# Attention and a routed expert network on one core: expert tiles fetch their own weights, second product two tiles late, segments of 10 and 6 blocks

## The chip, the cores and the metric

The kernel runs on one core of a Trainium2 chip. A core has five engines with a queue each: PE (TensorE, matrix products), DVE (VectorE), ACT (ScalarE), POOL (GpSimd) and SP (SyncE, which here only issues transfers). Transfers issued by SP, ACT and POOL are carried out by 16 DMA engines. The metric is the device time of one execution in microseconds; lower is better.

## The reference, cut to what matters

The input x has 16 sequences ("blocks") of 512 rows of 128 numbers, 8192 rows ("tokens") in all.

```python
# 1. causal attention, 16 heads of 8
Q, K, V = x@Wq, x@Wk, x@Wv
x1 = layernorm(x + softmax(mask(Q K^T / sqrt(8))) V @ Wo + bo)
# 2. two of eight experts for each token
xn = layernorm(x1) * gamma + beta
top1, top2, their probabilities -> weights g1, g2 (g1 + g2 = 1)
y_e = gelu(xn @ W1[e] + b1[e]) @ W2[e] + b2[e]      # 128 -> 512 -> 128
# 3.
out = layernorm(x1 + x1 + g1*y_top1 + g2*y_top2)
```

Each token needs only the two experts that it is routed to, so 16384 (token, expert) rows go through the expert network.

## The kernel before, in words

**Attention.** For each of the 16 blocks one iteration of some 44 us computes scores, exponentials and values, and two to three iterations later the block's rows are normalized, routed and written. POOL writes each normalized row twice by an indirect transfer into `rows_d` in DRAM, at the place that its expert's list has reached. Each row has 128 numbers and, as number 129, where its result belongs.

**Segments.** The lists are kept for two groups of blocks ("segments"), 0 to 11 and 12 to 15. When a segment's blocks are routed, DVE works out a plan (`plan_part`): which 128 rows of `rows_d` each tile reads and which expert it belongs to. Segment 0 has 104 tiles of 128 rows, segment 1 has 40, together 144 (`NT`). Lists that don't end at 128 are filled by `pad_ends`, eight transfers of SP for each segment.

**Expert tiles.** Tile n passes the engines so. SP (`load_tile`, L461 to L473) reads the tile's row number from `plan_i` into a register (L472) and starts the transfer of 128 rows to `xs`, eight tiles ahead, into one of twelve slots; before that it waits until the slot's former tile has been sent (L471). PE transposes the tile (`turn_tile`, L1122). DVE copies the transposed tile (`turned`, L1488), and copies the expert's first weights (128 x 512) from `w1_s`, which holds those of all experts, to one of two slots `w1_t` (`weights`, L1480). PE multiplies (`first_product`, L1132, four products of 128 x 128 x 128), ACT adds the bias b1 and applies gelu (L840), PE multiplies with W2 from `w2_s` one tile later (`second_product`, L1148), DVE adds the bias b2 (`result`, L1496), and POOL sends the 128 result rows to `y_d` by an indirect transfer (`send`, L640). DVE reads the expert's number into a register twice for each tile (`expert_of`, L1473), ACT once (L834), PE once (L1140).

`w1_s` lies in the memory of the attention's keys (`kside`), `w2_s` in that of its queries (`qarea`); both are filled in block 15's iteration (`load_experts`).

**Order.** Each engine's program is one list. Tiles 0 to 85 are written between the instructions of the attention's last three iterations (16 to 18, in which blocks 14 and 15 are finished), two to each of the 16 head steps from step 5 of iteration 16; the others follow in the loop over STEPS. In step n PE does first_product(n), turn_tile(n + 2), second_product(n - 1); DVE weights(n + 1), turned(n + 2), result(n - 1); POOL send(n - 1); SP load_tile(n + 8). `store_attention` (eight transfers, L397) and `load_attention` (one, L406) of block 15 stand on SP's list at head steps 8 and 11 of iteration 16.

**Last stage.** For each block SP loads 512 KB of `y_d` and 256 KB of `x2_d` (L509, L511), DVE adds the two choices (L1523, eight instructions) and takes statistics (L1533, L1539), POOL works out one over the deviation in eight small steps (`zrstd`, L691 to L699), ACT normalizes (L855), SP stores (L515). Block b begins with step 108 + 3b: twelve blocks begin beside tiles, the four of segment 1 after the last tile.

In rows of the profile the digits of names are left out: `w_t` is `w1_t`, `w_d` is `w1_d` or `w2_d`, `x_d` is `x2_d`, `b_s` is `b1_s`. `vpad` holds the gelu's output, the transposed tiles and the results, `ring`, `ps_v` and `ps_m` are PSUM, and `probs` holds the data of the last stage.

## Time and profile before

| | us |
|---|---|
| median of 3 runs | 1116.17 (1111.87 to 1117.45) |
| the profiled execution | 1118.13 |
| its span (first to last instruction) | 1116.4 |
| busy in the span: PE, DVE, ACT, POOL | 966.8, 830.4, 665.9, 683.8 |
| first transfer of a tile issued | 746.24 |
| first product of tile 0 | 750.37 |
| end of the last second product | 1080.95 |
| tile stage, between these two | 330.6 |
| from there to the end of the span | 35.4 |

The profiled execution took 2 us more than the median. Shares of busy time are means over the whole; the change touches the part from block 15's iteration on, so the views that count are those cut to that part: busy time by stretches, waits by engine, and instructions in order of time.

### The profile page before, as it was taken

How to read it: one execution, taken by the hardware profiler on the slowest of the kernel's cores; microseconds unless marked ns; L12 is line 12 of the kernel's file. 1: busy time of each engine (PE TensorE's matmuls, PEld its weight loads, DVE VectorE, ACT ScalarE, POOL GpSimd, SP SyncE). 2: the span in 40 equal slices, each digit the busy share in tenths (PEclk: the TensorE clock that was granted, in tenths of full speed). 3: DMA queues.
4: the chain of work that ended last, by engine and by line, in shares of the span. 5: the costliest groups of instructions: out<-in, count | busy, mean ns of one | idle time of the engine just before them, and what ended most of it. 6: DMA issues, size and time to landing. Idle time of an engine off the chain costs nothing.

```text
span 1116.4 us, 29852 instructions
## 1 busy us (share of the span) xinstructions
PE 966.8 (87%) x9185; PEld 640.2 (57%) x9185; DVE 830.4 (74%) x2262; ACT 665.9 (60%) x1338; POOL 683.8 (61%) x1063
## 2 busy tenths in 40 slices
PE   3789999999999989999999999879899889998750
PEld 1344454454545545544455455349899879997740
DVE  4777878888888898898888888974455455467744
ACT  1256657666666676676666766646475745556552
POOL 7022445775766766756657667666668546557874
PEclk9699999999999999999999999979899999999985
DMA  7523133143242342432432423343222223265515
GB/s 168 186 74 115 57 96 121 50 138 102 65 137 91 87 128 64 121 122 51 138 101 66 134 74 98 117 139 89 71 73 71 78 67 87 71 200 183 166 54 169
DMA packets 134569, 117.75 MB, mean 105 GB/s; under 512 B 56218, under 2 KB 99777, under 8 KB 134240
## 3 DMA queue, kind: packets, MB, share of 16 engines
q1 hardware_dynamic: 121808, 96.37, 29.7%
q0 software_dynamic: 8704, 17.06, 4.5%
q10 hardware_dynamic: 3904, 2.43, 0.9%
q8 instruction: 78, 1.28, 0.5%
q14 instruction: 75, 0.61, 0.2%
HBM read 65.26 MB, written 53.81 MB: 107 GB/s over the span
## 4 chain that ended last, share of the span: by engine, by line
PE 43%; DVE 18%; POOL 11%; issue 10%; ACT 7%; DMA 6%; SPq 4%; ACTq 1%; DVEq 0%; POOLq 0%
PE ring L1132 9%; PE ring L1148 9%; DVE negmax L1192 8%; PE ps_v L1072 5%; PE ring L1009 4%; PE ring L1040 4%; ACT probs L730 3%; POOL probs L598 2%; PE ring L1055 2%; SPq L397 2%; POOL rows_d L610 2%; PE ps_m L937 2%; POOL y_d L640 2%; DMA rows<-att_d 2%; PE ps_m L902 2%
## 5 line engine op out<-in xcount | busy, mean ns | idle before, releaser
L730 ACT ACTIVATE probs<-ring 128x768 f32<-128x768 f32 (+1 forms) x384 | 337.3, 883 | 213.5 <-PE ring L1009 212.5
L1192 DVE TENSOR_REDUCE negmax<-ring 128x2 f32<-128x1024 f32 (+3 forms) x512 | 409.3, 812 | 67.5 <-PE ring L1055 63.8
L598 POOL TENSOR_SCALAR_AFFINE_SELECT probs<-probs 128x512 f32<-128x512 f32 x256 | 163.6, 639 | 247.5 <-ACT probs L730 245.4
L840 ACT ACTIVATE vpad<-ring,b_s 128x128 f32<-128x128 f32 x576 | 165.0, 371 | 107.8 <-PE ring L1132 105.9
L640 POOL DMA_INDIRECT y_d<-vpad,xs x144 | 146.1, 1015 | 102.3 <-DVE vpad L1496 75.4
L1009 PE MATMUL ring<-qarea,kside 64*128 64x512 f32 (+3 forms) x1024 | 178.6, 387 | 24.0 <-DVE negmax L1192 18.0
L1040 PE MATMUL ring<-kside,qarea 64*128 64x256 f32 (+2 forms) x1024 | 166.5, 363 | 28.8 <-ACT probs L730 15.1
L1009 PEld LDWEIGHTS ring<-qarea,kside 64*128 64x128 f32 x1024 | 87.3, 187 | 179.3 <-issue 118.8
L1072 PE MATMUL ps_v<-probs,vpad 128*32 128x512 f32 (+3 forms) x2048 | 180.4, 448 | 1.8 <-POOL probs L598 1.8
L1148 PE MATMUL ring<-qarea,vpad 128*128 x1152 | 157.5, 280 | 20.1 <-ACT vpad L840 20.0
L1132 PE MATMUL ring<-vpad,w_t 128*128 128x128 f32 x1152 | 157.1, 280 | 8.8 <-issue 8.6
L1148 PEld LDWEIGHTS ring<-qarea,vpad 128*128 128x128 f32 x1152 | 140.6, 192 | 26.8 <-issue 24.4
L1132 PEld LDWEIGHTS ring<-vpad,w_t 128*128 128x128 f32 x1152 | 142.1, 194 | 13.5 <-issue 13.0
L610 POOL DMA_INDIRECT rows_d<-xn,slot x128 | 129.1, 1009 | 25.9 <-issue 24.7
L1055 PE MATMUL ring<-pastb,diagb 64*128 64x128 bf16 (+1 forms) x1536 | 126.6, 244 | 0.0
L1040 PEld LDWEIGHTS ring<-kside,qarea 64*128 64x128 f32 x1024 | 88.9, 190 | 43.2 <-ACT probs L730 23.7
L1480 DVE COPY w_t<-kside 128x512 f32 x144 | 65.4, 454 | 54.0 <-PE ring L1132 42.5
L1496 DVE TENSOR_TENSOR vpad<-ring,xin 128x128 f32<-128x128 f32 x144 | 41.9, 291 | 83.1 <-PE ring L1148 74.6
L1055 PEld LDWEIGHTS ring<-pastb,diagb 64*128 64x128 bf16 x1536 | 45.5, 97 | 55.6 <-issue 40.3
L1072 PEld LDWEIGHTS ps_v<-probs,vpad 128*32 128x32 f32 x2048 | 44.8, 109 | 44.8 <-issue 35.1
L855 ACT ACTIVATE probs<-probs,zrs 128x128 f32<-128x128 f32 x64 | 27.6, 492 | 44.1 <-POOL zrs L699 44.1
L1523 DVE SCALAR_TENSOR_TENSOR probs<-probs,gates 128x128 f32<-128x128 f32 x128 | 35.9, 342 | 11.9 <-DMA probs<-x_d 11.7
(178 smaller groups left out, 1162.8 us busy)
## 6 DMA issues: line engine op xcount, KB each, us to landing
qk_d<-qarea SPq DMA_DIRECT2D x62, 256.0 KB, 2.6
kside<-qk_d SPq DMA_DIRECT2D x96, 128.0 KB, 3.0
qarea<-qk_d SPq DMA_DIRECT2D x90, 128.0 KB
xs<-rows_d SPq DMA_DIRECT2D x144, 66.0 KB, 1.9
probs<-y_d SPq DMA_DIRECT2D x16, 512.0 KB
xin<-L_attn_x SPq DMA_DIRECT2D x16, 256.0 KB, 3.0
att_d<-attt SPq DMA_DIRECT2D x128, 32.0 KB
rows<-att_d SPq DMA_DIRECT2D x16, 256.0 KB
```

The costliest lines, as they stand in the source:

```text
L598: pool.affine_select(out=diag, in_=diag, pattern=[[0, 4], [1, P]], compare_op=ALU.is_ge, fill=0.0, base=0, channel_multiplier=-1).then_inc ...
L610: pool.indirect_dma_start(rows_d, bass.IndirectOffsetOnAxis(ap=slot[:, late.parity, k, q:q + 1], axis=0), xn[:, late.parity, q, k, :], Non ...
L640: pool.indirect_dma_start(y_d, bass.IndirectOffsetOnAxis(ap=xs[:, n % RING, D:D + 1].bitcast(I32), axis=0), ys[:, n % RING, :], None, boun ...
L730: nc.scalar.activation(of_unit(h // 2, part), ring[:, 2 * part % 3, :, (0, P, P)[part]:S], ACT.Exp, scale=SCALE).then_inc(sem("exp_done"), 1)
L840: ins = nc.scalar.activation(ht[:, n % 4, c, :], ps_a[:, n % 4, c * P:(c + 1) * P], ACT.Gelu_apprx_tanh, bias=b1_s[:, bass.ds(e, 1), c:c + ...
L1009: ins = pe.matmul(ring[:, 2 * n % 3, half, c0:c0 + S - q0], kside[rows, i.parity, e, g, kb * P:(kb + 1) * P], qside[i.parity][rows, g, q0: ...
L1040: pe.matmul(ring[:, (2 * n + 1) % 3, half, c0:c0 + nk], qside[b.parity][rows, g, qb * P:(qb + 1) * P], kside[rows, b.parity, e, g, 0:nk], ...
L1055: ins = pe.matmul(to, diagb[rows, at:at + P], past, start=False, stop=(c == 1))
L1072: ins = pe.matmul(ps_v[32 * j:32 * j + 32, kb * P:S], vpad[:, b.parity, kb, h, :], of_block(h, kb), start=(g % 2 == 0 and kb == 0), stop=( ...
L1132: ins = pe.matmul(ps_a[:, n % 4, c * P:(c + 1) * P], w1_t[:, n % 2, c * P:(c + 1) * P], xst[:, n % 4, :], start=True, stop=True)
L1148: ins = pe.matmul(ps_s[:, n % 2, 0:D], ht[:, n % 4, c, :], w2_s[:, bass.ds(e, 1), c, :].rearrange("p a d -> p (a d)"), start=(c == 0), sto ...
L1192: ins = nc.vector.tensor_reduce(negmax[:, n // 6 % 2, qb, s:s + 2], ring[:, (2 * n + 1) % 3, :, c0:c0 + nk], AX.X, ALU.max, negate=True)
```

## The change

1. The expert's first weights, both biases and the rows now come by transfers from one DRAM array. A table `table_d` has for each expert and partition a line of 644 numbers (`LINE`): 512 of W1, 4 of b1, 128 of b2. `load_tile` reads two numbers by one load of registers from `plan_o` (offset of the rows, offset of the table's part) and starts two transfers: 66 KB of rows to `xs` and 322 KB (128 x 644 x 4 bytes, 330 thousand bytes) to `w_t`, now a ring of twelve slots in the keys' memory. DVE's copy of the weights and the register loads of DVE and ACT are gone.
2. The table is written at the start: W1 with a stride, b2 repeated for 128 partitions, b1 by four transfers of 1024 numbers of 4 bytes. Loading W1 and b2 in block 15's iteration, and turning b1, are gone. From slot 6 on the weights' ring lies in memory that block 15 reads, so load 6 waits for its last scores.
3. second_product, result and send come two tiles late (`LAG`), not one.
4. Segments are blocks 0 to 9 (88 tiles) and 10 to 15 (56 tiles). Blocks 0 to 9 begin their last stage with steps 94 + 5b, the six of segment 1 after the last tile, with step 146 + 3k.
5. In the last stage POOL's `zrstd` handles two blocks at once (blocks 14 and 15 alone), DVE instead of ACT normalizes blocks 0 to 7 (`last_norm`, 4 instructions for a block), and stores stand later on SP's list.
6. The exponentials of the gates of blocks 14 and 15 are put off to after the last tile (`late_exponentials`, `late_gates`), block 15's `load_attention` stands at head step 9 and not 11.

```diff
-    FIRST = (0, NB - 4, NB)
+    FIRST = (0, NB - 6, NB)
...
+    LAG = 2
+    LATE = NB - 2
+    LINE = F + FC + D
...
+        w_t = kflat[:, 0:RING * LINE].rearrange("p (r c) -> p r c", r=RING)
...
-        LAST0, LAST_STEP, LAST_PARTS = TILE0[1] + 4, 3, 12
+        LAST0, LAST_PARTS = TILE0[1] + 4 + LAG, 20
+        BEGIN = [LAST0 + 5 * b if b < FIRST[1] else NT + LAG + 3 * (b - FIRST[1]) for b in range(NB)]
...
-            sp.dma_start(w1_d, w1).then_inc(sem("experts_out"), 16)
+            sp.dma_start(table_d[:, :, 0:F], w1).then_inc(sem("experts_out"), 16)
+            sp.dma_start(table_d[:, :, F + FC:LINE], b2.unsqueeze(1).broadcast_to([E, P, D])).then_inc(
+                sem("experts_out"), 16)
+            for c in range(FC):
+                sp.dma_start(table_d[:, :, F + c], b1[:, c * P:(c + 1) * P],
+                             allow_slow_non_contiguous=True).then_inc(sem("experts_out"), 16)
...
-                row = sp.value_load(plan_i[0:1, 0, m:m + 1], min_val=0, max_val=BASE[1] + E * REG[1] + E * P - P)
-                sp.dma_start(xs[:, m % RING, :], rows_d[bass.ds(row, P), :]).then_inc(sem(f"tile_in{m % RING}"), 16)
...
+                if m == EARLY:
+                    sp.wait_ge(sem("scores_ready"), UNITS * NB)
+                    sp.wait_ge(sem("max_scores"), AUNITS * NB)
+                _, values = nc.values_load_multi_w_load_instructions(
+                    plan_o[0:1, m, :], engines=(mybir.EngineType.SP,), min_val=0,
+                    max_val=ROWS * ROW + (E - 1) * P * LINE)
+                sp.dma_start(xs[:, m % RING, :], both_d[bass.ds(values[0], P * ROW)].rearrange(
+                    "(p c) -> p c", p=P)).then_inc(sem(f"tile_in{m % RING}"), 16)
+                sp.dma_start(w_t[:, m % RING, :], both_d[bass.ds(values[1], P * LINE)].rearrange(
+                    "(p c) -> p c", p=P)).then_inc(sem(f"table_in{m % RING}"), 16)
...
-                        if h == 11:
+                        if h == 9:
                             load_attention(sp, i.plus(-1))
...
-                    if b is not None:
+                    if b is not None and b >= BY_ACT:
                         last_norm(b, part)
...
-                if 0 < n <= NT:
-                    second_product(n - 1)
+                if LAG <= n < NT + LAG:
+                    second_product(n - LAG)
...
             def tile(n):
-                if n + 1 < NT:
-                    weights(n + 1)
                 if n + 2 < NT:
                     turned(n + 2)
-                if 0 < n <= NT:
-                    result(n - 1)
+                if LAG <= n < NT + LAG:
+                    result(n - LAG)
```

How rows stand on SP, which issues the tiles' transfers, late in the tile stage. Before, one store of a finished block, a tile's load, the loads of a block for the last stage, and the next tile's load:

```order
L515 DMA out<-probs 128x4x128
L472 TENSOR_LOAD plan_i
L472 ISA x2
L473 ISA
L473 DMA xs<-rows_d 128x132
L509 DMA probs<-y_d 128x1024
L511 DMA probs<-x_d 128x512
```

Now, in the same part (`kside` is the memory in which the weights' ring lies):

```order
L508 DMA kside<-both_d 128x644
L549 DMA out<-probs 128x4x128
L503 TENSOR_LOAD plan_o
L503 ISA x4
L506 REGISTER_ALU
L506 DMA xs<-both_d 128x132
L508 REGISTER_ALU
```

For each tile SP had four kinds of rows, one of them a transfer; it has the load, four register steps, two single ones and two transfers.

How rows stand on DVE in the last part of the tile stage, where a block's last stage runs beside the tiles. Before:

```order
L1496 TENSOR_TENSOR vpad<-ring,xin 128x128
L1533 BN_STATS zst<-probs 128x6 x4
L1473 TENSOR_LOAD plan_i
L1473 ISA x2
L1480 ISA
L1480 COPY w_t<-kside 128x512
L1488 COPY vpad<-ps_v 128x128
```

Now:

```order
L1540 TENSOR_TENSOR vpad<-ring,kside 128x128
L1577 BN_STATS zst<-probs 128x6 x4
L1592 TENSOR_SCALAR probs<-probs,zrs 128x128
L1533 COPY vpad<-ps_m 128x128
```

The copy of 128 x 512 and the register loads have left DVE; a normalizing instruction of the last stage has come to it.

## Rows read from the trace of the kernel before

**Rows 1.** Busy time by stretches: stretch, length, five engines' busy us, clock, DMA share, GB/s.

```profile
960.00:980.00 20.00, 20.00 (x181) 20.00 (x181) 9.69 (x33) 12.52 (x44) 10.74 (x11) 1.00 0.25 70
1000.00:1020.00 20.00, 19.05 (x162) 18.24 (x161) 17.35 (x79) 13.28 (x44) 15.69 (x27) 1.00 0.64 197
1020.00:1040.00 20.00, 14.78 (x123) 13.74 (x122) 13.49 (x60) 12.08 (x40) 15.46 (x29) 1.00 0.59 186
1090.00:1100.00 10.00, 0.00 (x0) 0.00 (x0) 6.47 (x28) 1.66 (x4) 3.05 (x10) 0.50 0.95 329
```

**Rows 2.** Instructions in order of time, two first products of the undisturbed tile stage.

```profile
968.20 1.06 PE L1132 MATMUL ring<-vpad,w_t 128*128 128x128 f32 x8
...
970.10 1.06 PE L1132 MATMUL ring<-vpad,w_t 128*128 128x128 f32 x8
```

**Rows 3.** PE's instructions, 750 to 1081 us, by line: busy, mean ns, idle before.

```profile
L1148 PE MATMUL ring<-qarea,vpad 128*128 x1152 | 157.5, 280 | 20.1 <-ACT vpad L840 20.0
L1132 PE MATMUL ring<-vpad,w_t 128*128 128x128 f32 x1152 | 157.1, 280 | 8.8 <-issue 8.6
L937 PE MATMUL ps_m<-wo_s,rows 128*128 128x128 f32 x8 | 2.0, 437 | 3.8 <-DMA rows<-att_d 3.8
```

**Rows 4.** PE's waits, 1000 to 1090 us: us in total, times, longest.

```profile
PE ring L1148 <- ACT vpad L840: 13.0, 8, 2.5
```

**Rows 5.** A register load of DVE (min/median/max ns), then groups of instructions by line.

```profile
L1473 DVEq TENSOR_LOAD <-plan_i x288: 297/302/650, 748.2 to 1077.6; - x144
...
L1480 DVE COPY w_t<-kside 128x512 f32 x144 | 65.4, 454 | 54.0 <-PE ring L1132 42.5
L1496 DVE TENSOR_TENSOR vpad<-ring,xin 128x128 f32<-128x128 f32 x144 | 41.9, 291 | 83.1 <-PE ring L1148 74.6
L1523 DVE SCALAR_TENSOR_TENSOR probs<-probs,gates 128x128 f32<-128x128 f32 x128 | 35.9, 342 | 11.9 <-DMA probs<-x_d 11.7
...
L640 POOL DMA_INDIRECT y_d<-vpad,xs x144 | 146.1, 1015 | 102.3 <-DVE vpad L1496 75.4
```

**Rows 6.** SP's instructions for one tile's load: ns min/median/max.

```profile
L472 SPq TENSOR_LOAD <-plan_i x144: 262/268/412, 745.5 to 1058.3; - x144
L472 SPq FUSED_REGOPS  x144: 152/152/159, 745.8 to 1058.6; - x144
...
L473 SPq DMA_DIRECT2D xs<-rows_d x144: 337/338/1190, 746.2 to 1059.0; - x144
```

**Rows 7.** SP's transfers in order of time: start, us from first to last, count.

```profile
735.20 8.99 SPq L459 DMA_DIRECT2D rows_d<-zrow  x8
746.24 8.08 SPq L473 DMA_DIRECT2D xs<-rows_d  x8
...
764.00 6.26 SPq L397 DMA_DIRECT2D att_d<-attt  x8
...
780.47 1.54 SPq L406 DMA_DIRECT2D rows<-att_d  x1
```

**Rows 8.** The chain that ended last, its part at the kernel's end: start, us, what.

```profile
1081.66 0.28 POOL zrs L691
...
1084.55 0.21 POOL zrs L699
...
1086.67 2.10 DMA y_d<-vpad,xs
...
1089.37 3.96 DMA probs<-x_d
...
1100.50 1.03 DVE probs L1523 x4
...
1104.01 1.03 DVE probs L1523 x4
```

**Rows 9.** The chain that ended last, the first product of tile 0.

```profile
750.58 1.73 PE ring L1132 x8
```

**Rows 10.** Transfers by line: count, KB each, us from issue to landing.

```profile
wgt<-L_ffn_Wg SPq DMA_DIRECT2D x1, 4.0 KB, 5.7
```

More of the change, by code:

```diff
@@ L633, in body @@
                     for n in expert_steps(i, h):
-                        send(n - 1)
+                        send(n - LAG)
             def send(n):
@@ L700, in zrstd @@
                     if k:
-                        pool.wait_ge(sem("zrstd"), 7 * b + k)
+                        pool.wait_ge(sem("zrstd"), 7 * GROUPS.index(group) + k)
                     step().then_inc(sem("zrstd"), 1)
             for n in STEPS:
-                send(n - 1)
+                send(n - LAG)
                 b = last_stage(n, 4)
-                if b is not None:
-                    zrstd(b)
+                if b is not None and b == GROUPS[group_of(b)][-1]:
+                    zrstd(GROUPS[group_of(b)])
         @block.scalar
@@ L1294, in route @@
             def route(b, n):
-                if not b.exists(NB):
+                if not b.exists(NB) or (n >= 15 and b.value >= LATE):
                     return
@@ L1302, in route @@
                         dve.wait_ge(sem("zrow_ready"), 1)
-                if n == 1:
+                if n == 1 and b.value < LATE:
                     need(dve, sem("gate_exp"), 2, b, 0)
@@ L1555, in _ @@
                     last_statistics(b)
+                for k in range(2 * QB):
+                    b = last_stage(n, 7 + k)
+                    if b is not None and b % 2 and b < BY_ACT:
+                        last_norm(b - 1 + k // QB, k % QB)
 def kernel(**inputs):
```

182 lines of the change are left out of this document (104 added, 78 removed).

## The prediction, made before the changed kernel was run

> **What bounds the kernel now.** I read first the busy time by stretches, since the shares of the whole say nothing about the part that changes. Between 960 and 980 us PE is busy without a gap, 181 instructions in 20 us at the full clock [rows 1], and a first product starts 1.90 us after the one before [rows 2]. So an undisturbed tile costs 1.90 us and PE sets it. The same view from 1000 us on shows PE at 162 and then 123 instructions in 20 us while POOL is busy 15.5 of 20 and DVE 13.5 [rows 1]: there something else sets the pace. Second I read PE's waits: in that stretch 13.0 us in 8 waits for ACT's gelu in front of the second product [rows 4], over the whole stage 20.1 us there, 8.6 us of short waits in front of the first product, and one of 3.8 us for the block 15 attention rows (`rows<-att_d`) [rows 3]. The gelu itself is late because ACT stands behind its normalizing, which waits for POOL, which stands between sends. Third, SP's list in order of time [rows 7], because the change puts its new work there.
>
> The floor of the tile stage: 144 x 1.90 = 273.6 us, plus PE's remaining instructions of attention and routing; one of their larger groups is 2.0 us busy [rows 3], with all the others I take 7. Together 281, against 330.6 taken. About 50 us are lost in the stage, and the question is how many of them the change gives back and what it puts in their place.
>
> **The change part by part.**
>
> *DVE.* It loses 144 copies of 454 ns and 288 register loads of 302 ns [rows 5], whose steps stand in front of the copies. Per tile there remain the copy of the transposed tile (the same size as the result's, 0.29) and the result, 0.29, together 0.58 us. A block of the last stage costs 8 x 0.34 = 2.7 for the two additions [rows 5] and, by the chain at the end, 3.5 us in all with its statistics, from the start of one block to the next [rows 8]. Before, one block per 3 tiles gave 1.2 + 1.0 plus the register loads, over 2.3 us for a tile. Now one per 5 tiles gives 0.7, and four normalizing instructions, which the trace of before doesn't show on DVE: between 0 and the 0.34 us of the addition of the same size, taken 0.25, so 0.2 per tile. Sum 1.5 us, under PE's 1.90. The short waits in front of the first product go, except some 2 us where DVE works out the second plan in small dependent steps, which is still there.
>
> *POOL.* A send takes 1.02 us [rows 5], with the idle time around it 1.3; `zrstd`, 3.1 us from its first to its last step [rows 8] and some 4 where it is disturbed, comes once for 2 blocks in 10 tiles instead of once in 3. That is 2.6 us per tile before, which alone explains the pace after 1000 us, and 1.7 now.
>
> *ACT and LAG.* The gelu gets a whole tile more before PE wants it, the Exp tables no longer come between gelus, and ACT does no normalizing for blocks 0 to 7. The 20.1 us of waits [rows 3] should go entirely. Nothing is late behind them but what follows.
>
> *SP's queue* takes the new work. A load of a tile took 8.08 / 8 = 1.01 us [rows 7], of which 0.27 + 0.15 + 0.34 are the register load, its step and the issue [rows 6]. New are one more register step of 0.15, a second issue (0.34 for one by register, up to 0.78, the 6.26 / 8 of `att_d<-attt` [rows 7]), and gaps between seven instead of four instructions. Between 0.5 and 1.0 us more, so 1.5 to 2.0; I take 1.67, since the second transfer is addressed as the first. That is under 1.90, but hardly. Where SP has other work, it falls behind:
> - at the start: eight loads from 746.2 to 759.6 instead of 754.3, then six more until about 770, then the eight attention stores of 6.3 us. Tile 14 is issued near 777 and lands near 780, while PE wants it at about 775.5. This wait of 4.5 us takes the place of the 3.8 us wait for the attention rows, though these are asked for two steps earlier;
> - `pad_ends` of the second segment: 9 us as for the first [rows 7], against a lead of about 8: 2 us;
> - the burst of four blocks' loads, 3.1 MB, which at 329 GB/s [rows 1] takes 9.5 us of all DMA engines, with tiles' loads queued behind it. Before, it met a lead of 6 tiles and cost nothing. Now I give it 4 us (0 to 9);
> - in the last stage three more transfers a block, 1.4 us in 5 tiles, so 1.95 per tile against 1.90: 44 tiles, 2.5 us.
>
> The Trainium skill ("DMA: Bandwidth & Descriptors", Issuing engines are not separate DMA queues) says that the sequencer's time to start a transfer is usually small relative to the transfer. Here a load costs SP 1.01 us, and 66 KB at the 329 GB/s seen later are 0.2 us, so this trace says the opposite for small transfers. By the page's rule the four entries above but the burst would vanish, and the time would be 9 us lower than my sum.
>
> *DMA.* A tile moved 132 KB at a share of 0.25, that is 0.47 us of all engines [rows 1]. The weights add 330 KB, at 329 / 0.95 = 346 GB/s 0.95 us: 1.4 of 1.90. In the last stage a block's 1.05 MB add 210 KB a tile, 0.6 us: 2.0 us at its worst. The eight tiles of lead even this out over the last eight tiles, which load nothing; I cost it with the burst.
>
> *The start.* Table, biases and their small transfers come where before two copies of 4 MB ran; of b1 there are four transfers of 1024 numbers of 4 bytes. The nearest row, `wgt`, has 1024 such numbers and lands in 5.7 us [rows 10]. Nobody waits for these transfers, but they share the engines with the first blocks' transfers. Bounds 0 and 5.7, for one such delay on the chain; taken 1, since they are issued far ahead of block 1's. The first tile waits for two transfers: 0.5 us.
>
> *PE's clock.* The first product of tile 0 took 1.73 us on the chain [rows 9] where 1.06 is usual [rows 2]: after a wait the granted clock is lower for a few products. For the start and one wait I leave 4 us, as before.
>
> *The end.* From PE's last product to the end it was 35.4 us. Of it 5.3 us the last send stood behind `zrstd` on POOL; now the zrstd of blocks 8 and 9 stands before the last two sends, 4 us. After the sends come 4 us of loading and then 3.5 us of DVE for each block [rows 8], six blocks instead of four: +7.0. Sum 35.4 - 1.3 + 7.0 = 41.1, so +5.8 with rounding.
>
> *The sum.* Tile stage 281 + 4 (clock) + 4.5 + 2 + 2 + 4 + 2.5 = 300.0, that is 30.6 less. With +5.8, +1 and +0.5 the change is -23.3 us. On the profiled execution 1118.1 - 23.3 = 1094.8; on the median 1116.2 - 23.3 = 1093. I take 1094.
>
> **The rivals.**
> - *Everything is hidden.* If SP's load costs 1.5 us, it keeps its lead, and the wait at tile 14, the pads, the burst and the last stage cost nothing: 13 us less, and another 3 us if `zrstd` no longer holds the last sends: 1078. For it: the median issue of 0.34 us; against: three long runs of other transfers on the same queue.
> - *SP is the new bound.* If the second issue takes 0.6 to 0.78 us and its register steps are not overlapped, a load costs 2.0 us. Then 144 x 2.0 = 288 and another 6.3 + 9 + 14 us of attention stores, pads and last-stage transfers stand on the same queue: about 317 for the stage, 17 more than the sum: 1111. For it: every other issue of this queue with long rows took 0.43 us or more.
>   The Trainium skill ("DMA: Bandwidth & Descriptors", Latency and other measured facts) gives a floor of about 600 ns for a `tensor_load`. With it a load would cost 0.33 us more, 2.0 as in this rival; the trace shows 268 ns [rows 6], so the measured value stands.
> - *The DMA engines become the bound, and it is slower than before.* In the last stage 670 KB must move per tile. At the 70 / 0.25 = 280 GB/s that the small packets reach now [rows 1] this takes 2.4 us, with waits of transfers on one another 2.6: 50 tiles x 0.7 = 35 us over the floor instead of 6.5, and the rows' 528-byte packets late in the earlier tiles too: about 1125. It decides below 285 GB/s in the last stage (the 23 us of gain spread over 50 tiles make 2.36 us a tile). Against it: 197 GB/s at a share of 0.64 is 308 for a full share, and 329 were reached [rows 1].
> - *Half the gain.* The waits for the gelu go, but in the last stage DVE's 1.5 us a tile are really 2.1, as its small instructions wait for one another: 50 tiles x 0.2 = 10 us more, 1104.
>
> **How the numbers follow.** My forecast, 1086 to 1102, has 0.45. All hidden, 1072 to 1086, 0.17. SP as the bound or half the gain, 1102 to 1117, 0.24. DMA as the bound, over 1117, 0.14. The range of 8 in 10 is 1077 to 1117. A measurement of this kernel can tell about 0.5%, 5.6 us, from no change: faster is below 1110.6, which is the first two, and over half of the third, 0.77; within 0.5% 0.11; slower 0.12.
>
> **What would show it.** In the profile after: first products 1.90 us apart between tiles 30 and 70, and 1.9 to 2.0 in the last stage; no wait of PE for the gelu; SP's tile loads 1.6 to 1.75 us apart in the first eight; one wait of PE of 3 to 6 us for the rows of tile 14 and none for the attention rows; the tile stage 296 to 304 us; the end 40 to 43 us with six blocks 3.5 us apart. It is wrong if the loads are 1.9 us apart or more (SP is the bound), or if PE waits for `w_t` in the last stage with a DMA share over 0.9. It is also wrong if block 1's start comes over 3 us later than before.

## The result, and the profile after

The changed kernel is slower: 1145.6 us (median of 4 runs, 1144.6 to 1152.4) against 1116.8 us for the kernel before on the same chip, ratio 1.0274 with a 95% interval of 1.024 to 1.0309. The forecast was 1094 us. The profiled execution has a span of 1143.3 us against 1116.4. By the instructions in order of time it splits into three stretches:

| stretch | before | after | change | forecast |
|---|---|---|---|---|
| start to first product of tile 0 | 750.4 | 755.7 | +5.3 | +1.5 |
| first product to end of last second product | 330.6 | 344.7 | +14.1 | -30.6 |
| from there to the end of the span | 35.5 | 43.0 | +7.5 | +5.8 |
| sum, us | 1116.4 | 1143.3 | +26.9 | -23.3 |

The chain that ended last, page of the changed kernel, its shares by engine. In the kernel before SP's queue (SPq) had 4% of this chain:

```profile
PE 27%; SPq 22%; DVE 18%; issue 12%; POOL 8%; DMA 7%; ACT 5%; ACTq 0%; POOLq 0%; DVEq 0%
```

SP's waits, 760 to 1090 us (us in total, times, longest), first of before, where SP waited 115 us for a slot to come free, then of after, where this is its only wait:

```profile
SPq L472 <- DMA y_d<-vpad,xs: 115.3, 86, 4.9
```

```profile
SPq L503 <- DMA y_d<-vpad,xs: 0.8, 1, 0.8
```

So SP issues without a pause from the first tile to the last, and everything behind it goes at its pace. What a tile costs it, by its three lines, min/median/max ns (to compare with [rows 6]):

```profile
L503 SPq FUSED_REGOPS  x288: 147/147/159, 750.3 to 1089.7; - x144
L503 SPq SEQ_ASSERT  x288: 18/18/23, 750.5 to 1089.9; - x144
L503 SPq TENSOR_LOAD <-plan_o x144: 462/475/1419, 749.8 to 1088.0; - x144
```

```profile
L506 SPq ALU_OP  x144: 33/37/55, 750.8 to 1090.0; - x144
L506 SPq MOVE xs<-both_d x144: 29/29/38, 750.9 to 1090.0; - x144
L506 SPq DMA_DIRECT2D xs<-both_d x144: 332/333/552, 751.0 to 1090.1; - x144
```

```profile
L508 SPq DMA_DIRECT2D kside<-both_d x144: 328/333/1155, 751.5 to 1090.6; - x144
```

The register load of two values takes 475 ns where that of one took 268 [rows 6], and the bounds step of 147 + 18 ns comes twice. With two issues of 333, two address steps of 37 and two moves of 29 (L508 has one of each too) that is 475 + 330 + 666 + 132 = 1603 ns. With the gaps between these eleven instructions a load comes every 2.03 us. The list of SP's transfers in order of time shows the distance, and what happens when other work stands on the queue:

```profile
751.00 0.37 SPq L506 DMA_DIRECT2D xs<-both_d  x1
751.53 0.35 SPq L508 DMA_DIRECT2D kside<-both_d  x1
753.07 0.33 SPq L506 DMA_DIRECT2D xs<-both_d  x1
...
755.09 0.33 SPq L506 DMA_DIRECT2D xs<-both_d  x1
...
778.96 0.33 SPq L508 DMA_DIRECT2D kside<-both_d  x1
779.41 5.35 SPq L427 DMA_DIRECT2D att_d<-attt  x8
785.97 0.35 SPq L506 DMA_DIRECT2D xs<-both_d  x1
...
927.58 0.33 SPq L506 DMA_DIRECT2D xs<-both_d  x1
928.08 0.72 SPq L508 DMA_DIRECT2D kside<-both_d  x1
929.58 8.17 SPq L487 DMA_DIRECT2D both_d<-zrow  x8
939.00 0.35 SPq L506 DMA_DIRECT2D xs<-both_d  x1
```

From 751.00 the last of the 144 loads, at 1090.1, is 339.1 us away, and 143 distances of 2.03 us are 290.3 of it. Three large intervals add 5.5 (attention stores), 9.4 (the pads of the second segment) and 5.0 us (the first loads of the last stage), the rest comes in pieces of 0.1 to 3.5 us. Since SP has no lead that is not used up, each of them is paid in full. PE's waits, same stretch:

```profile
PE ps_v L1160 <- DMA xs<-both_d: 13.9, 6, 6.4
PE ring L1184 <- issue: 11.6, 24, 0.8
PE ring L1170 <- DVE vpad L1533: 7.2, 1, 7.2
PE ps_m L1160 <- DMA xs<-both_d: 2.5, 1, 2.5
```

No wait for the gelu is among them; there were 20.0 us of it [rows 3]. PE now waits for the tiles' rows. The wait of 7.2 us names DVE, but DVE stood still itself, 9.5 us in front of the first block of the last stage, for the burst of loads (`DVE probs L1567 <- DMA probs<-x_d: 9.5, 1, 9.5` in DVE's waits). The stretches of [rows 1], after (columns as there):

```profile
960.00:980.00 20.00, 19.41 (x167) 18.56 (x166) 5.26 (x18) 11.40 (x40) 8.43 (x9) 1.00 0.76 210
1000.00:1020.00 20.00, 18.25 (x145) 17.70 (x144) 9.70 (x45) 9.58 (x34) 12.24 (x17) 0.91 0.86 255
1020.00:1040.00 20.00, 16.63 (x142) 15.79 (x141) 12.37 (x56) 10.27 (x36) 12.61 (x17) 0.99 0.87 254
```

At 1020 PE does 142 instructions in 20 us where it did 123, with DVE and POOL less busy: the relief of these engines came as forecast. But at 960, where it did 181, it does 167. PE is still counted as 97% busy there, though it does 8% fewer instructions in the same time. That fits a tile every 2.03 us instead of 1.90: the share of busy time doesn't show that PE is fed too slowly, the count of instructions does.

The start. SP's first transfers, in order of time:

```profile
29.48 16.29 SPq L463 DMA_DIRECT2D both_d<-L_ffn_b  x4
45.81 1.85 SPq L465 DMA_DIRECT2D w_d<-L_ffn_W  x1
47.78 0.51 SPq L380 DMA_DIRECT2D xin<-L_attn_x  x1
```

b1's four transfers of 4-byte runs hold SP for 16.3 us. W2's copy, which went out at 27.95 before, now goes out at 45.8, and block 2's input at 47.8 instead of 28.6 (it lands 12.0 us later). Right behind them stands the first store of block 1's keys into `qk_d`. It is issued only 0.5 us later than before, but on the chain that ended last it takes 6 us longer to land. First the kernel before, then the changed one:

```profile
51.83 2.08 DMA qk_d<-qarea
```

```profile
52.34 8.07 DMA qk_d<-qarea
```

The end, on the chain that ended last of after (to compare with [rows 8]). The last send is again issued behind a `zrstd` chain, 4.3 us after the one before it:

```profile
1099.60 0.97 POOL y_d L675
1100.59 0.28 POOL zrs L727
...
1104.85 0.33 POOL y_d L675
...
1106.26 2.09 DMA y_d<-vpad,xs
```

Then six blocks of the last stage follow on DVE, first and last here in order of time; four more lie between them, 3.5 to 3.8 us apart:

```profile
1112.82 2.31 DVE L1567 SCALAR_TENSOR_TENSOR probs<-probs,gates 128x128 f32<-128x128 f32 x8 [4.82 <-DMA probs<-x_d]
...
1130.75 2.28 DVE L1567 SCALAR_TENSOR_TENSOR probs<-probs,gates 128x128 f32<-128x128 f32 x8
```

### The profile page after: what moved, and what is told of

Its sections match the earlier page's. It is cut to its first block, busy times and chain, and to the rows that moved or that the text cites. A ratio compares the mean times of both kernels' runs of the same rounds, so it can differ in the third digit from the quotient of the medians.

```text
span 1143.3 us, 28185 instructions
## 1 busy us (share of the span) xinstructions
PE 973.8 (85%) x9184; PEld 647.3 (57%) x9184; DVE 791.6 (69%) x2150; ACT 643.2 (56%) x1297; POOL 660.5 (58%) x1007
## 4 chain that ended last, share of the span: by engine, by line
PE 27%; SPq 22%; DVE 18%; issue 12%; POOL 8%; DMA 7%; ACT 5%; ACTq 0%; POOLq 0%; DVEq 0%
SPq L503 8%; DVE negmax L1228 8%; PE ps_v L1112 5%; PE ring L1049 5%; SPq L508 4%; SPq L506 4%; PE ring L1080 4%; ACT probs L766 2%; PE ring L1184 2%; POOL probs L633 2%; POOL both_d L645 2%; PE ring L1095 2%; DVE rv L1330 2%; PE ring L1170 2%; SPq L427 2%
## 5 line engine op out<-in xcount | busy, mean ns | idle before, releaser
L873 ACT ACTIVATE vpad<-ring,kside 128x128 f32<-128x128 f32 x576 | 164.2, 368 | 170.1 <-PE ring L1170 169.1
L675 POOL DMA_INDIRECT y_d<-vpad,xs x144 | 143.0, 993 | 139.7 <-DVE vpad L1540 106.9
L1184 PE MATMUL ring<-qarea,vpad 128*128 x1152 | 164.0, 288 | 13.1 <-issue 11.6
L1170 PE MATMUL ring<-vpad,kside 128*128 128x128 f32 x1152 | 159.0, 283 | 7.2 <-DVE vpad L1533 7.2
L1184 PEld LDWEIGHTS ring<-qarea,vpad 128*128 128x128 f32 x1152 | 146.6, 200 | 22.9 <-issue 22.2
L1170 PEld LDWEIGHTS ring<-vpad,kside 128*128 128x128 f32 x1152 | 146.5, 200 | 7.4 <-DVE vpad L1533 7.4
L645 POOL DMA_INDIRECT both_d<-xn,slot x128 | 128.9, 1007 | 29.4 <-issue 27.1
L1540 DVE TENSOR_TENSOR vpad<-ring,kside 128x128 f32<-128x128 f32 x144 | 42.0, 292 | 107.9 <-PE ring L1184 106.6
L1533 DVE COPY vpad<-ps_v 128x128 f32<-128x128 f32 x116 | 33.7, 291 | 80.1 <-PE ps_v L1160 78.6
L1160 PE MATMUL ps_v<-ident,xs 128*128 128x128 f32 x116 | 33.5, 289 | 16.5 <-DMA xs<-both_d 15.6
L1567 DVE SCALAR_TENSOR_TENSOR probs<-probs,gates 128x128 f32<-128x128 f32 x128 | 36.2, 346 | 14.7 <-DMA probs<-x_d 14.5
```

The source lines that it names most:

```text
L645: pool.indirect_dma_start(rows_d, bass.IndirectOffsetOnAxis(ap=slot[:, late.parity, k, q:q + 1], axis=0), xn[:, late.parity, q, k, :], Non ...
L675: pool.indirect_dma_start(y_d, bass.IndirectOffsetOnAxis(ap=xs[:, n % RING, D:D + 1].bitcast(I32), axis=0), ys[:, n % RING, :], None, boun ...
L873: ins = nc.scalar.activation(ht[:, n % 4, c, :], ps_a[:, n % 4, c * P:(c + 1) * P], ACT.Gelu_apprx_tanh, bias=w_t[:, n % RING, F + c:F + c ...
L1170: ins = pe.matmul(ps_a[:, n % 4, c * P:(c + 1) * P], w_t[:, n % RING, c * P:(c + 1) * P], xst[:, n % 4, :], start=True, stop=True)
L1184: ins = pe.matmul(ps_s[:, n % 2, 0:D], ht[:, n % 4, c, :], w2_s[:, bass.ds(e, 1), c, :].rearrange("p a d -> p (a d)"), start=(c == 0), sto ...
```

## Experiments

Theory: SP's queue is the bound of the tile stage (2.03 us a load against 1.90 of PE), and b1's transfers are the late start. Rivals: the weights' bytes (45 MB more, DMA share 0.76 to 0.87 in the stretches above), and what came with the table (lag of two, segments, last stage).

The experiments form four groups on four chips. All kernels of a group share a chip, and ratios are always to the kernel before on that chip. It took 1116.8 us on the chip of the result, 1149.8, 1147.3 and 1149.6 us on the chips of the first, second and fourth group, and 1118.1 on that of the third. So absolute times are compared within a group, and an expectation in microseconds that was worked out from another chip (in e1 to e4, e10 and e11) has to be read as a ratio. How the chips differ is told in the section on unexpected things. In the tables the first load is the start of tile 0's transfer of rows, the tile stage runs from the first first product to the end of the last second product, and the tail from there to the end.

**First group: each suspect alone.**

*e1: the bounds steps of SP's register load left out.*

```
     _, values = nc.values_load_multi_w_load_instructions(
         plan_o[0:1, m, :], engines=(mybir.EngineType.SP,), min_val=0,
-        max_val=ROWS * ROW + (E - 1) * P * LINE)
+        max_val=ROWS * ROW + (E - 1) * P * LINE,
+        skip_runtime_bounds_check_because="offsets are clamped in the plan")
```

> The changed kernel without the four register steps (two times an operation of 147 ns and one of 18) with which SP checks the two offsets of each tile against their bounds; the offsets themselves are the same. SP theory (in the changed kernel SP's list sets the pace: a load every 2.03 us, 1.60 us of it instructions, the rest gaps between them): a load takes some 1.6 us, which is under PE's 1.90 us a tile, PE is the bound again, the tile stage shrinks from 343 to 300 to 315 us and the time falls from 1146 to 1105 to 1120. DMA theory (the 16 DMA engines set the pace: they are 0.8 busy in the tile stage): the loads queue up behind one another, landing times grow, and the time stays within 5 us of 1146.

*e2: of a table line only the last 132 columns are transferred* (66 KB instead of 322; W1's columns in the slot are never written).

```
-    sp.dma_start(w_t[:, m % RING, :], both_d[bass.ds(values[1], P * LINE)].rearrange(
-        "(p c) -> p c", p=P)).then_inc(sem(f"table_in{m % RING}"), 16)
+    sp.dma_start(w_t[:, m % RING, F:LINE], both_d[bass.ds(values[1], P * LINE)].rearrange(
+        "(p c) -> p c", p=P)[:, F:LINE]).then_inc(sem(f"table_in{m % RING}"), 16)
```

> The changed kernel with only 132 of the 644 numbers of each table line transferred (the two biases), so the first weights are not loaded at all and the output is not the reference's; SP's instructions are the same in kind and number. SP theory: loads stay 2.0 us apart and only the waits go in which transfers pile up (the burst of four blocks' loads), 1146 falls by 0 to 10 us. DMA theory: with 66 instead of 322 KB of weights a tile the share of the DMA engines falls from 0.8 to under 0.45, the bound is gone, and the time falls to 1115 or lower.

*e3: b1 by one transfer with runs of 16 bytes* (its numbers then stand in another order).

```
-    for c in range(FC):
-        sp.dma_start(table_d[:, :, F + c], b1[:, c * P:(c + 1) * P], ...)
+    sp.dma_start(table_d[:, :, F:F + FC], b1.rearrange("e (p c) -> e p c", c=FC)).then_inc(
+        sem("experts_out"), 16)
```

> The changed kernel with b1 written into the table by one transfer with runs of 16 bytes (1024 of them) in place of four transfers with 4096 runs of 4 bytes; the hidden units get one another's biases, so the output is not the reference's. Start theory (the four transfers hold SP for 16.3 us and the DMA engines beyond 52 us, so that the keys of block 1 land in 8.1 instead of 2.1 us and everything after is about 5 us late): the store of block 1's keys lands in 2 to 4 us, the first tile's load is issued near 747 instead of 751, and the time falls by 4 to 6 us to about 1141. Rival (the start is late because of the strided copy of W1 or the second copy of W2): no change.

*e4: the table taken back*: one dynamic transfer of rows, W1's copy and both register loads of DVE as before; lag of two, segments of 10 and 6 and the new last stage kept.

> The changed kernel without its table: weights by DVE's copy, biases and register loads of DVE and ACT, and SP's single transfer for a tile as before; second product two tiles late, segments of 10 and 6, the last stage and the late gates as changed. If the waits for the gelu and POOL's small steps were what was lost before (my forecast of the other parts): the tile stage takes 295 to 310 instead of 330 us, the end 42 to 45 instead of 35, so the time is 1096 to 1108 against 1116 before. Rival (DVE, with 2.1 us of copies, register loads and last stage a tile, is then the bound): stage 320 to 330, time 1115 to 1123.

Measured:

| kernel | us | ratio, interval | first load | tile stage | tail |
|---|---|---|---|---|---|
| e1 | 1136.2 | 0.9888 (0.984 to 0.9936) | 748.0 | 339.8 | 42.5 |
| e2 | 1172.1 | 1.023 (1.018 to 1.028) | 750.5 | 370.4 | 42.6 |
| e3 | 1165.9 | 1.0162 (1.012 to 1.0204) | 745.9 | 369.8 | 42.7 |
| e4 | 1147.0 | 0.9977 (0.9954 to 1.0) | 742.4 | 354.1 | 42.1 |

e2 moves a fifth of the weights' bytes, and its tile stage is as long as e3's with all of them. Busy time by stretches of e2, where the DMA share has fallen to 0.35:

```profile
860.00:920.00 60.00, 54.30 (x447) 51.74 (x448) 17.38 (x79) 29.30 (x103) 30.80 (x33) 0.97 0.35 92
```

SP has no wait of its own in e2 either, but for one of 0.3 us. The bytes are not the cause: e3, with all of them, has the same tile stage on the same chip. e1 leaves out only instructions of SP's queue and is 36 us faster than e2. Its SP waits again, 18.7 us for slots in 760:1090:

```profile
SPq L503 <- DMA y_d<-vpad,xs: 18.7, 21, 4.5
```

e3, with b1 in one transfer, is 6.2 us faster than e2: its first load is 4.6 us earlier, its tile stage 0.6 us shorter. On the chain of e3 the store of block 1's keys lands in 2.08 us again.

e4 says that everything but the table makes together no difference that can be seen, where 1096 to 1108 us against 1116 had been expected; read as a ratio it is near the rival named there, 1115 to 1123. That is a gain and a loss that cancel: against the kernel before on a chip of the same kind (second group: tile stage 364.4, tail 33.6) its tile stage is 10 us shorter and its tail 8.5 us longer.

**Second group: the same chip for before and after, and two other ways.** The two kernels themselves:

> The kernel before, run as one of the kernels of this call, so that its trace stands beside the others on one chip. Both theories expect a ratio of 1.00 (0.995 to 1.005). What it is to tell: in the call before this one the kernel before took 1149.75 us instead of 1116.17. If that chip is just slower in the tile stage, the trace shows the tile stage (first product to last second product) longer than 330.6 us with the attention part as it was (first tile transfer at about 742 to 746 us). If the chip is the one of the first call, the stage is about 331 us.

> The changed kernel as it stands. If SP's queue is its bound, its loads stand 2.0 to 2.06 us apart on any chip, and the tile stage is close to 345 us, longer by about 5 where the chip has stalls of its own; ratio to before 1.01 to 1.03. Where the kernel before loses time in the tile stage to such stalls, and the changed one hides some of them under SP's pace, the ratio comes nearer to 1. If the weights' bytes were the bound instead, the stage would change with what the transfer engines give on that chip, and the loads would not keep one distance.

*e5: e1's edit and b1 in one transfer with the right order*: hidden unit 4p+c in chunk c, W2 split the same way, and W1's columns read with a stride.

```
-    ins = pe.matmul(ps_a[:, n % 4, c * P:(c + 1) * P], w_t[:, n % RING, c * P:(c + 1) * P],
+    ins = pe.matmul(ps_a[:, n % 4, c * P:(c + 1) * P], w_t[:, n % RING, c:F:FC],
                     xst[:, n % 4, :], start=True, stop=True)
```

> The changed kernel with both costs of SP taken out: no runtime bounds steps behind the load of the two offsets, and b1 put into the table by one transfer with runs of 16 bytes, hidden unit 4p+c in chunk c (the first product reads its weights with a stride of 4 values, W2 is loaded by the same split). If SP's queue is the cause of the loss and b1's runs of 4 bytes are the late start: loads 1.65 to 1.7 us apart, first tile load 4 to 6 us earlier than in the changed kernel, ratio to before 0.980 to 0.989, that is 4 to 6 us below the one without bounds steps alone (0.9888). If TensorE pays for weights read with a stride, the weight loads of the first product grow and the ratio is above 0.99. If the tile stage is bound by bytes after all, it stays above 1.01.

*e6: e4 with the bounds steps of all register loads of the tile stage left out* (SP, ACT, PE, two on DVE), by the same argument as in e1.

> The kernel without the table (one dynamic transfer of rows, W1's copy by DVE, second product two tiles late, segments of 10 and 6), with the bounds steps behind every register load of the tile stage (SP, ACT, PE and two on DVE for each tile) left out. The kernel with the steps had 0.9977. If those loads' steps lie on the path of a tile (two loads in a row on DVE, one ahead of the gelu, one ahead of the second product), about 0.3 us per tile on DVE goes and up to 20 of the 353 us of the tile stage, ratio 0.98 to 0.99. If PE and the order of its waits set the stage, the ratio stays at 0.995 to 1.0.

Measured: before 1148.9 us, ratio 1.0011 (0.9984 to 1.0039), tile stage 364.4; after 1168.5, ratio 1.0196 (1.016 to 1.0233), tile stage 369.2; e5 1209.3, ratio 1.0567 (1.0522 to 1.0612), tile stage 418.2; e6 1139.5, ratio 0.9942 (0.9921 to 0.9963), tile stage 345.2. The tail of after is 42.6 us here too (before: 33.6), and its first load at 750.0 stands 7.3 us behind that of before (742.7). e6 has 0.35% less than e4 relative to before, with intervals that touch: without the table bounds steps are worth little. e5 missed its main expectation (0.980 to 0.989) by far; the other one named there, the price of the stride, came true. Weight loads and products by line, and two first products in order of time:

```profile
L1170 PEld LDWEIGHTS ring<-vpad,kside 128*128 128x128 f32 x936 | 227.4, 327 | 0.0
L1184 PEld LDWEIGHTS ring<-qarea,vpad 128*128 128x128 f32 x936 | 113.7, 192 | 0.6 <-issue 0.6
```

```profile
852.25 2.03 PE L1170 MATMUL ring<-vpad,kside 128*128 128x128 f32 x8
...
855.12 2.03 PE L1170 MATMUL ring<-vpad,kside 128*128 128x128 f32 x8
```

A weight load of every fourth number takes 327 ns beside 192 ns for the contiguous ones of the second product, and a tile 2.87 us instead of 1.90 [rows 2]. PE waits 0.2 us in all between 760 and 1090 us: it is the bound.

**Third group: SP's steps out, and one part changed at a time.** Its chip is like that of the result (before 1118.1 us). The three kernels have e1's edit, and b1's four transfers are taken from the start and stand behind what SP issues for the last attention block.

```
                 body_sp(sp, i)
                 if not i.loop and i.value == NB - 1:
+                    for c in range(FC):
+                        sp.dma_start(table_d[:, :, F + c], b1[:, c * P:(c + 1) * P], ...)
                     load_experts(1)
+                    sp.wait_ge(sem("experts_out"), 16 * (3 + FC))
```

> The changed kernel without the runtime bounds steps behind the load of the two offsets, and with b1's four transfers of 4-byte runs moved from the start of the program to the last block of the attention, behind what SP issues for that block and ahead of its waits for W2's room. If these transfers held SP for 16 us at the start and cost the program what the late first tile load shows (749.97 against 742.68 in the kernel before, and 745.89 with b1 in runs of 16 bytes), the first tile load comes 3 to 6 us earlier than without that move, and the time is 3 to 6 us below that of the kernel that leaves out the bounds steps alone: ratio to before 0.983 to 0.987, against 0.9888. If the transfers cost the same wherever they stand (their room on the DMA engines, or a wait for them ahead of the first tile), the ratio stays at 0.987 to 0.992.

e8 adds `FIRST = (0, NB - 4, NB)`, `LAST0 + 3 * b` and `BY_ACT = 0`; e9 adds to e7 only `LAG = 1` (the last stage's steps, counted from `LAG`, move up by one with it).

> The kernel of the last one, with segments of 12 and 4 blocks as before the change instead of 10 and 6, the last stage's blocks every 3 tile steps, and all of its norms by ACT. The tail behind the last second product holds four blocks of the last stage instead of six, at 3.5 us each: if the split is what the tail costs, it falls from 42.5 to about 35.5 us. What it can cost in the tile stage: blocks at three steps' distance share the tiles' time with DVE and ACT, bounds 0 to 8 us. Net ratio to before 0.976 to 0.987 if the tail's gain is kept, 0.987 to 0.995 if the tile stage gives it back.

> The kernel without bounds steps and with b1's transfers late, with the second product one tile late instead of two. PE then waits for the gelu of the tile just before: in the kernel before that was 13.0 us of waits for ACT in 1000:1090 and 20.1 in all. If the lag of two is what took them away, 15 to 30 us come back: ratio to before 0.998 to 1.012. If the gelu waits were an effect of DVE's load (which the table takes off, by which ACT gets its input earlier), the lag is worth under 5 us and the ratio is 0.983 to 0.99.

| kernel | us | ratio, interval | first load | tile stage | tail |
|---|---|---|---|---|---|
| e7 | 1109.6 | 0.9928 (0.9903 to 0.9954) | 756.8 | 305.9 | 42.9 |
| e8 | 1105.4 | 0.9897 (0.9863 to 0.9931) | 755.7 | 306.2 | 35.2 |
| e9 | 1107.6 | 0.9907 (0.987 to 0.9944) | 755.1 | 308.4 | 38.1 |

In e7 the tile stage is 305.9 us, 39 less than in the changed kernel: with loads 1.5 to 1.6 us apart it gets a lead, waits for slots again, and between 800 and 860 PE is busy without a gap, with all the weights' bytes moving.

```profile
SPq L500 <- DMA y_d<-vpad,xs: 25.0, 27, 2.7
```

```profile
800.00:860.00 60.00, 60.00 (x543) 59.99 (x543) 21.80 (x94) 38.67 (x133) 45.33 (x58) 1.00 0.83 239
1000.00:1090.00 90.00, 63.02 (x547) 61.10 (x545) 53.54 (x239) 41.06 (x139) 51.17 (x70) 0.89 0.81 258
```

What PE still waits for in 760:1090 is 8.2 us for the tiles' rows, 5.1 us for DVE at the burst of the last stage, where the stretch 960:980 has a DMA share of 1.00 at 361 GB/s, and 1.3 us for the attention rows. Moving b1's transfers gained nothing, against the expectation of a ratio of 0.983 to 0.987: the late start went from block 1 to the end of the attention (first load 756.8 instead of 751.0), since the pads and first loads are queued behind them.

e8's tail is 35.2 us, as long as that of before: six blocks instead of four behind the last tile cost 7.7 us, and the tile stage doesn't give it back (306.2). Its ratio and e7's overlap; e8 also moved the norms to ACT and the last stage's blocks to every third step, so the tail, not the time, is the result. e9 says the lag is worth nothing that can be seen once the table has relieved DVE: PE's waits for the gelu are 8.1 us (6.1 in one) where e7 has 0.5, and the tile stage is 2.5 us longer, but the tail is 4.8 us shorter, as the last result comes a tile earlier and the last send waits for it alone, no longer for a `zrstd`.

```profile
PE ring L1186 <- ACT vpad L875: 8.1, 3, 6.1
```

The counterpart is e4, with the lag of two and no table. In the same stretch its wait for the gelu is 1.8 us; the kernel before on such a chip (second group) has 12.2. First the kernel before, then e4:

```profile
PE ring L1148 <- ACT vpad L840: 12.2, 13, 1.6
```

```profile
PE ring L1187 <- ACT vpad L871: 1.8, 3, 0.7
```

So the table without the lag and the lag without the table, each with the new last stage, take more than half of these waits away. Which of them ended the waits in the changed kernel can't be said.

**Fourth group: the two causes apart.** b1's transfers are taken from the start and stand behind what SP issues for block 0, in a pause of SP that is there in the kernel before too.

```
                 body_sp(sp, i)
+                if not i.loop and i.value == 0:
+                    for c in range(FC):
+                        sp.dma_start(table_d[:, :, F + c], b1[:, c * P:(c + 1) * P], ...)
```

> The changed kernel with one edit: b1's four transfers of 4-byte runs stand behind what SP issues for block 0, where SP of the kernel before is idle from 64 to 86 us, instead of at the start of the program. If they cost the program their 16.3 us of SP's queue at the start (and gave a first tile load about 5 us late), the first tile load comes back to 745 to 747 us and the time falls 4 to 6 us below the changed kernel: ratio to before 1.021 to 1.024 where the changed one had 1.0274. The loads stay 2.03 us apart. If their cost is on the DMA engines wherever they stand, the ratio stays at 1.026 to 1.030.

> The same, and the runtime bounds steps behind the load of the two offsets left out. If SP's queue is the bound, its loads go from 2.03 to 1.57 us apart where it doesn't wait, the tile stage from 345 to 306 us as in the kernel with b1's transfers late (1109.55 us, first tile load at 756.8), and the first tile load stands at 745 to 748 us: 1098 to 1102 us, ratio to before 0.982 to 0.987. If the late first load of that kernel was no effect of b1's transfers, it is 0.990 to 0.995.

> The same with segments of 12 and 4 blocks, the last stage's blocks every 3 tile steps, its norms by ACT. With b1's transfers late this split gave 1105.38 against 1109.55 us, and a tail of 35.2 against 42.9 us. If the tail is what the split sets, the gain of 4 to 8 us stays: 1092 to 1098 us, ratio to before 0.977 to 0.983. If the two were chance of the DMA order, no difference to the kernel with 10 and 6.

> The same as the one before, with TensorE's register load for the second product (one value for each tile) also without bounds steps. TensorE waited 5.9 us in all for its own issue there in 760:1090 (12 times, longest 0.7 us). If this is time on its path, up to 6 us go, ratio 0.002 to 0.005 below the one before; if weight loads ahead cover it, no difference.

| kernel | us | ratio, interval | first load | tile stage | tail |
|---|---|---|---|---|---|
| e12 | 1164.0 | 1.0131 (1.0083 to 1.0178) | 742.9 | 370.4 | 42.6 |
| e10 | 1131.6 | 0.9829 (0.9793 to 0.9865) | 740.8 | 339.6 | 43.5 |
| e11 | 1130.8 | 0.9815 (0.978 to 0.9851) | 743.4 | 348.4 | 34.9 |
| e13 | 1123.6 | 0.9769 (0.9723 to 0.9816) | 744.1 | 337.0 | 35.0 |

e12 has the first load back at 742.9, where it is in the kernel before (742.7 in the second group, on a chip of the same kind). Its time is not apart from the changed kernel's by the ratios (1.0131 and 1.0196, whose intervals overlap), the first load is. In the pause the same four transfers hold SP for 5.3 us instead of 16.3. At the start, behind the table's copies, even the one transfer of W2 holds it for 8.8 us; what holds an issue there is not shown:

```profile
29.15 8.76 SPq L462 DMA_DIRECT2D w_d<-L_ffn_W  x1
38.01 0.97 SPq L380 DMA_DIRECT2D xin<-L_attn_x  x1
...
64.23 5.26 SPq L514 DMA_DIRECT2D both_d<-L_ffn_b  x4
```

Block 2's input goes out 9.4 us later than in the kernel before and costs nothing, and the store of block 1's keys lands in 2.08 us. So the late input is not what made the start late; that nothing is in the way of the keys' store is what counts.

e10 against e12 is the bounds steps alone, on one chip: 32.4 us, of which 30.8 in the tile stage. Undisturbed loads came 2.03 us apart and now come 1.52 to 1.57, so 144 of them are some 66 us less on SP's queue; half of that is gained; then SP waits for slots again (22.7 us in all), so something else sets the pace. The forecast of 306 us for the tile stage came from the third group's chip; the ratio lies in the expected 0.982 to 0.987. e11 against e10 is no difference: its tail is 8.6 us shorter, its tile stage 8.8 longer. On this chip the last stage at three steps a block costs what the tail gives; in the third group it did not. e13 against e11 has 7 us for PE's bounds steps; the intervals touch, so the size is open. e13 has the lowest ratio found, 0.9769 with an interval of 0.9723 to 0.9816: it is faster than the kernel before, by about 2%.

## Why the prediction was wrong, point by point

- **The step that failed is SP's load.** Taken 1.67 us, bounds 1.5 to 2.0, measured 2.03. The 0.36 us fall into three parts, each rounded. First, the round of the kernel before was read too short: 8.08 us from the start of the first to the end of the eighth issue [rows 7] hold seven rounds and one issue of 0.34, so a round was (8.08 - 0.34) / 7 = 1.11 us and not 8.08 / 8 = 1.01. That is 0.10. Second, the load of two values was costed at the 268 ns of one value and takes 475: 0.21. Third, the small steps: the text added one register step of 0.15 and counted seven instructions. There are eleven, and the order of rows shown ahead of the prediction had nine of them; the second assert, address step and move add 0.06. The second issue (333 ns) and the added gaps (0.17) were as taken. With the right round alone the working gives 1.77 us, still under PE's 1.90; with the right register load too it gives 1.97 and SP is the bound. So the two together turn the forecast, and an instruction whose operand changes shape must not be costed as unchanged.
- **The threshold was seen and the price of passing it was not.** The text says 1.67 is under 1.90, "but hardly", and priced 2.0 as a rival at 1111 us (with another one, chance 0.24). So the rival had the load right and the time 35 us too low. It gave 317 us for the tile stage: 288 for the loads and 29 for other transfers, 14 of them for the last stage. Measured are 290 for the loads, 5.5 for the attention stores, 9.4 for the pads, 34 for everything else, and 5.5 more, since the last product ends 10.2 us after the last load and the first starts 4.7 us after the first. Where the rival had 14 us there are the 5.0 us of the last stage's first loads and some 29 us of single transfers and short disturbances, which no lead absorbs any more. A queue that is the bound pays for every entry on it; the sum listed only the long ones.
- **The attention stores, pads and burst** were right as places. PE waits 2.9 us for rows behind the stores (taken 4.5), 6.4 behind the pads (taken 2) and 7.2 at the burst (taken 4, bounds 0 to 9). These waits are not a sum on their own, since SP is late everywhere.
- **The Trainium skill's sentence** ("DMA: Bandwidth & Descriptors", Issuing engines are not separate DMA queues) that the time to start a transfer is usually small relative to it is not borne out here either: a tile's two transfers cost SP 2.03 us, and the DMA engines are not full in that time (shares of 0.76 to 0.87 in the stretches above, 0.35 in e2 with the tile stage unchanged). The floor of about 600 ns that the Trainium skill gives for a `tensor_load` (same page, Latency and other measured facts) would have put SP's load on the right side of the threshold. The rows show 268 ns for one value and 475 for two, so the page is too high for both, but nearer to the load of two than the 268 ns that I used.
- **The start** was taken 1 us (bounds 0 to 5.7) and cost about 5: the first load is 4.8 us later than before, and in e12 it is back. It fits the way that was named, transfers that share the DMA engines with block 1's. What was wrong is that they were taken to be issued far ahead: b1's transfers hold SP until 45.8 us, and W2's copy and an input then go out right in front of the store of block 1's keys. How much of the store's 6 us is W2's copy and how much the rest of b1's runs is not shown. The copies of the kernel before were of 2 MB each, not 4. The text's own condition, block 1 over 3 us later, was met (its keys are stored at 60.4 instead of 53.9 us).
- **The relief of DVE, POOL and ACT held.** The gelu waits are gone, DVE is busy 12.4 of 20 us at 1020 where it was 13.5, POOL 12.6 where it was 15.5, and with SP's steps out (e7) the tile stage is 305.9 us against the forecast of 300.0. But the text gave the end of the gelu waits to the lag and to what ACT loses, and with the table the lag of two is worth no time that can be seen (e9); without the table the same parts gave 10 us of the tile stage (e4).
- **The tail** was taken +5.8 and is +7.5. The two further blocks are 7.7 us by e8, as priced (7.0). The `zrstd` in front of the last send was taken as 1.3 us cheaper; of that nothing is to be seen, and by e9 the lag of two is what brings it there.
- **The DMA engines as the bound** (over 1117 us, the only rival past the range's end) did not come: e2 excludes it. The measured time lay beyond the 1125 us at which that rival was put, by the mechanism of another one.

## What to carry to other kernels

When a change puts a second transfer on a queue, count every instruction of one round on that queue's engine, with the price of the operand's new shape, and compare with the round of the engine that sets the pace. While the queue is below it, its other entries are free; once it is above, each one is paid in full. So a load of 2.03 us beside a tile of 1.90 cost 39 us of the tile stage (e7 against the changed kernel, on two chips of one kind) and not 144 x 0.13 = 19. When a price is read from a run of issues in a row, n issues hold n - 1 rounds. Look for instructions to leave out on the queue (bounds steps of values that are clamped anyway) before taking the change back: the same table with 0.46 us less on SP for each load turned 1.013 into 0.983. And transfers in tiny runs belong where the queue pauses: four of them held it 16.3 us at the start and 5.3 us some 35 us later.

## What the runs showed of the hardware that was not expected

- A register load of two values takes 475 ns on SP, of one 268; its bounds step 147 + 18 ns for each value.
- TensorE's weight load from SBUF with a stride of four 4-byte numbers takes 327 ns instead of 192 (e5). A tile takes 0.97 us more, and the tile stage is 78 us longer than in e1, on another chip of the same kind. The Trainium skill ("SBUF — State Buffer", Door 1: The DMA port swizzle) says that fp32 can be read at a stride of up to 4 for free, and in the same place that a new line of 16 bytes for each access costs; for weight loads of fp32 the trace agrees with the second statement and not with the first.
- Chips differ in this kernel's tile stage and hardly elsewhere. On three of five the kernel before takes 1147 to 1150 us; of those it was traced on one, where the first tile load stands at 742.7 against 746.2, the tail is 33.6 against 35.5, but the tile stage is 364.4 against 330.6 us. In the records of such chips single instructions of SP are stretched to about 0.7 us, with others of near zero beside them; on the chip of the result SP's register steps have neither. SP's load in the changed kernel on such a chip, to be read against 147/147/159 above:

```profile
L503 SPq FUSED_REGOPS  x288: 3/147/715, 749.3 to 1114.0; - x144
```

What holds the engines there is open; nothing was tried that tells it. In the second group SP's time between loads has a median of 2.34 us where it is 2.05 on the chip of the result, and SP again has no lead, so the changed kernel loses by the same mechanism. Its ratio is smaller (1.0196 against 1.0274): its tile stage grew by 24.5 us, that of the kernel before by 33.8.
